# A Mamba block's back half kept with channels on the partitions

## What is computed

```python
u = layernorm(x, ln_w, ln_b); zxbcdt = u @ in_proj_w.T      # z 1024, xBC 1280, dt 16
dt = softplus(dt + dt_bias)                                 # one per token and head
xBC = silu(depthwise_conv4(xBC) + conv_b)                   # xs 1024, B 128, C 128
# per token: state = state*exp(dt*A) + (dt*x) B^T ; y = state C   (16 heads of 64 channels)
y = y + D * xs
y = y * silu(z)
y = y * rsqrt(mean(y*y) + EPS) * gamma
out = x + y @ out_proj_w.T
```

## Time and profile before

| | us |
|---|---|
| median of 3 runs | 3517.11 |
| lowest, highest | 3514.15, 3523.29 |
| the profiled execution, its own time | 3522.4 |
| its span, first to last instruction | 3521.1 |
| mean granted TensorE clock, share of full | 0.98 |

### The profile page before, as it was taken

The page is one execution under the profiler, slowest core; times in us unless marked ns, Lnnn a source line. Parts: engine busy times, 40 slices in busy tenths (PEclk is TensorE's granted clock), DMA queues, the critical chain, the costliest instruction groups (busy, mean ns, idle before and its releaser), DMA issues.

```text
span 3521.1 us, 63878 instructions
## 1 busy us (share of the span) xinstructions
PE 3307.2 (94%) x24154; PEld 1911.8 (54%) x24154; DVE 2695.3 (77%) x4854; ACT 2583.8 (73%) x4698; POOL 1812.2 (51%) x1355
## 2 busy tenths in 40 slices
PE   6799999999999999999769999999999999999997
PEld 4455555555555555555425555555555555555554
DVE  6688878788788798889867676776777777777764
ACT  6888888888998888887537656577666766666664
POOL 1233334433243442423447887876665775566655
PEclk9899999999999999999879999999999999999999
DMA  5344443445443534443367576787676877667664
GB/s 165 97 115 114 120 107 93 112 121 129 112 107 87 124 109 127 117 115 79 77 149 152 104 128 110 128 152 143 123 136 118 151 142 123 120 127 136 119 113 68
DMA packets 687315, 419.41 MB, mean 119 GB/s; under 512 B 566583, under 2 KB 603831, under 8 KB 676768
## 3 DMA queue, kind: packets, MB, share of 16 engines
q1 hardware_dynamic: 630688, 312.58, 40.1%
q0 software_dynamic: 56320, 102.75, 16.7%
HBM read 176.00 MB, written 101.71 MB: 79 GB/s over the span
## 4 chain that ended last, share of the span: by engine, by line
PE 75%; DVE 6%; DMA 6%; ACT 4%; issue 4%; POOL 3%; SPq 1%; another core or an unknown queue 0%; ACTq 0%; POOLq 0%; DVEq 0%
PE pair L1236 9%; PE pair L1311 9%; PE pair L1359 8%; PE pair L1281 8%; PE pair L1468 7%; PE pair L1321 6%; PE pair L1375 4%; PE pair L1390 3%; PE pair L1437 2%; PE pair L1436 2%; PE pair L1301 2%; PE pair L1292 2%; PE pair L1406 2%; DMA yT<-yhl 2%; PE pair L1456 1%
## 5 line engine op out<-in xcount | busy, mean ns | idle before, releaser
L1616 DVE SCALAR_TENSOR_TENSOR cv<-raw,taps,cv 128x512 f32<-128x512 f32 x480 | 433.0, 922 | 34.6 <-ACT cv L2010 31.1
L1861 DVE TENSOR_REDUCE smx<-pair 128x2 f32<-128x514 f32 x512 | 349.3, 685 | 55.8 <-PE pair L1406 53.2
L2281 POOL TENSOR_TENSOR ph<-pf,ph 128x1024 f16<-128x1024 f32 x128 | 291.5, 2277 | 185.8 <-ACT ph L2146 185.3
L1236 PE MATMUL pair<-xhT,whi 128*128 128x512 f16 x1280 | 382.2, 380 | 2.7 <-DVE yb L1686 1.0
L1311 PE MATMUL pair<-ohi,yT 128*128 128x512 f16 x1024 | 321.3, 386 | 26.3 <-DMA yT<-yhl 24.3
L2140 ACT ACTIVATE pf<-pair 128x1024 f32<-128x1024 f32 x256 | 261.8, 1023 | 113.9 <-PE pair L1437 95.4
L1281 PE MATMUL pair<-zhi,xhT 128*128 128x512 f16 x1024 | 327.3, 381 | 0.9 <-ACT btok L2030 0.4
L2040 ACT ACTIVATE de<-de,cum 128x128 f32<-128x128 f32 x1024 | 309.1, 388 | 0.4
L2146 ACT CAST ph<-pf 128x1024 f16<-128x1024 f32 x256 | 267.0, 1043 | 4.6 <-PE pair L1456 0.2
L2286 POOL TENSOR_TENSOR ohl<-of,ohl 128x256 f16<-128x256 f32 x256 | 209.8, 825 | 112.1 <-ACT ohl L2153 110.5
L1321 PEld LDWEIGHTS pair<-xdt,de 128*128 128x128 f32 x2048 | 241.3, 194 | 18.6 <-issue 12.5
(11 more groups left out here) (267 smaller groups left out, 9894.3 us busy)
## 6 DMA issues: line engine op xcount, KB each, us to landing
de<-cum SPq DMA_DIRECT2D x64, 1024.0 KB, 4.8
rows<-rowt SPq DMA_DIRECT2D x16, 1040.0 KB, 7.8
xin<-x SPq DMA_DIRECT2D x16, 1024.0 KB, 7.5
y<-xin SPq DMA_DIRECT2D x16, 1024.0 KB, 5.1
y<-ob POOLq DMA_DIRECT2D x64, 256.0 KB, 5.0
qb<-qa SPq DMA_DIRECT2D x32, 512.0 KB
rbc<-rank SPq DMA_DIRECT2D x63, 256.0 KB
wst<-wkv SPq DMA_DIRECT2D x32, 256.0 KB
```

Source lines behind the costliest of these rows:

```text
L1236: ins = pe.matmul(bk[:], w[:, k, ws], xt[:, ha, k, :], start=n == 0, stop=n == 3 * KD - 1)
L1616: ve.scalar_tensor_tensor(c_[:], r_[:, t:t + BLK], taps[:, ct, t:t + 1], c_[:], ALU.mult, ALU.add).then_inc(done, 1)
L1861: ve.tensor_reduce(smx[:, qt, 2 * h2:2 * h2 + 2], sc[:, :, 0:NK + 1], AX.X, ALU.max)
L2281: po.tensor_tensor(p_[:, 1], f[:], p_[:, 0], ALU.subtract).then_inc(S.plp, 1)
```

## The change

The back half keeps channels on the partitions. The intra product takes xdt of a head as the stationary operand (64 columns) and the decay matrix as the moving one, and two heads go to the two halves of the array's columns and of PSUM's partitions. z and inter exchange their operands. exp(cum) now varies along the free axis, so it comes by two broadcast DMAs per chunk (`ecb_in`) and one exp on ScalarE (`ecb`), into `ecb`. y is split before the norm, so `square`, `mean_` and `root` no longer stand ahead of the split; the DMA transpose `gate` is gone, and proj reads `ghl` directly. The sum of squares over the channels is a tree of three additions on GpSimd and one matmul with a single moving column (`norm`); its root scales the projection's output. The D term goes from VectorE to GpSimd, from `xsT`; the first tap from ScalarE to VectorE; the residual `skip` from ScalarE to GpSimd. `open_` leaves B out in the last chunk of a sequence. `state` moves ahead of intra. The planner's costs and dependences follow.

```diff
-          "POOL": {"low_p", "o_low", "weight_low", "row_low", "xw", "decayed", "y_skip"}}
+          "POOL": {"low_p", "o_low", "weight_low", "row_low", "xw", "decayed", "dxs", "y_skip", "tree"}}
...
 def back(i):
             if ch:
                 yield ("proj", ch - 1)
                 yield 5.18
+                yield ("norm", ch - 1)
+                yield 0.35
+            if not last and not ends(ch):
+                yield ("state", ch)
+                yield 1.72
             yield ("intra", ch)
-            yield 3.55
+            yield 1.95
...
 def z(ch, j):
-                n = 0
-                for k in range(KD):
-                    for ha, w in ((0, zhi), (0, zlo), (1, zhi)):
-                        pe.matmul(pz[:], xt[:, ha, k, cs], w[:, k, j * 512:(j + 1) * 512], start=n == 0, stop=False)
-                        n += 1
-                pe.matmul(pz[:], ones[:], z_bias[:, j * 512:(j + 1) * 512], start=False, stop=True).then_inc(S.z_mm, 1)
+                for m in range(KI // 2):
+                    ws, o, n = slice((KI // 2 * j + m) * P, (KI // 2 * j + m + 1) * P), pz[:, m * P:(m + 1) * P], 0
+                    for k in range(KD):
+                        for ha, w in ((0, zhi), (1, zhi), (0, zlo)):
+                            pe.matmul(o, w[:, k, ws], xt[:, ha, k, cs], start=n == 0, stop=False)
+                            n += 1
+                    ins = pe.matmul(o, z_bias[:, ws], ones[:], start=False, stop=True)
+                ins.then_inc(S.z_mm, 1)
 def inter(ch):
-                for j in range(2):
-                    ins = pe.matmul(pi[:, j * 512:(j + 1) * 512], xs[:, KI + 1, cs], sf[:, j * 512:(j + 1) * 512], start=True, stop=True)
+                for k in range(KI):
+                    ins = pe.matmul(pi[:, k * P:(k + 1) * P], sf[:, k * P:(k + 1) * P], xs[:, KI + 1, cs], start=True, stop=True)
 def intra(ch):
                 for h in range(NH):
-                    ins = pe.matmul(pw[:, h * HD:(h + 1) * HD], de[ch % 2][:, h, :], xdt[:, h, :], start=True, stop=True)
+                    k, a = divmod(h, 2)
+                    ins = pe.matmul(pw[a * HD:(a + 1) * HD, k * P:(k + 1) * P], xdt[:, h, :], de[ch % 2][:, h, :], start=True, stop=True)
+            def norm(ch):
+                q.wait_ge(S.tree, 3 * (ch + 1))
+                pe.matmul(bank("norm", ch)[:, 0:1], ysq[:, 0, :], upper[:, P - 1:P], start=True, stop=True).then_inc(S.nm_mm, 1)
 # VectorE
+            def tap0(i, ct):
+                ve.tensor_scalar(c_[:], r_[:, 0:BLK], taps[:, ct, 0:1], conv_bias[:, ct:ct + 1], ALU.mult, ALU.add).then_inc(S.cv0, 1)
-            def dxs_(ch):
-                ve.tensor_tensor(dxs[:], p3, d_bc[:].unsqueeze(2).to_broadcast([P, NH, HD]), ALU.mult).then_inc(S.dxs, 1)
 def y_low(ch):
-                ve.scalar_tensor_tensor(yhl[:, 1, :], yb[:].rearrange("p h d -> p (h d)"), yn[:, 2:3], yhl[:, 0, :],
-                                        ALU.mult, ALU.subtract).then_inc(S.yl, 1)
+                ve.scalar_tensor_tensor(ghl[:, 1], yb[:], GS, ghl[:, 0], ALU.mult, ALU.subtract).then_inc(S.yl, 1)
 # ScalarE
+            def ecb_(ch):
+                q.wait_ge(S.ecb_in, 32 * (fed(ch) + 1))
+                ac.activation(ecb[:], ecb[:], ACT.Exp).then_inc(S.ecb, 1)
 def square(ch):
-                ac.activation(yhl[:, 0, :], yf, ACT.Square, accum_out=yn[:, 0:1]).then_inc(S.sq, 1)
+                ac.activation(ysq[:], yb[:], ACT.Square).then_inc(S.sq, 1)
 # GpSimd
+            def skip(i, c):
+                po.tensor_tensor(xin[:, c, :], xin[:, c, :], xn[:], ALU.add).then_inc(S.skip, 1)
+            def dxs_(ch):
+                q.wait_ge(S.nm_mm, ch)
+                po.tensor_tensor(ysq[:], xsT[i % 2][:, 0:KI, c * P:(c + 1) * P], d_ch.unsqueeze(2).to_broadcast([P, KI, P]), ALU.mult).then_inc(S.dxs, 1)
+            def tree(ch):
+                q.wait_ge(S.sq, ch + 1)
+                po.tensor_tensor(ysq[:, 0:4], ysq[:, 0:4], ysq[:, 4:8], ALU.add).then_inc(*tree_own.up())
+                po.tensor_tensor(ysq[:, 0:2], ysq[:, 0:2], ysq[:, 2:4], ALU.add).then_inc(*tree_own.up())
+                po.tensor_tensor(ysq[:, 0], ysq[:, 0], ysq[:, 1], ALU.add).then_inc(*tree_own.up())
 # SyncE
-            def gate(ch):
-                sp.dma_start_transpose(yT[:], yhl[:].rearrange("p h d -> p (h d)")).then_inc(S.yT, 16)
+            def ecb_in(ch):
+                q.wait_ge(S.yi, fed(ch))
+                for a in range(2):
+                    sp.dma_start(ecb[a * HD:(a + 1) * HD], heads[a].partition_broadcast(HD)).then_inc(S.ecb_in, 16)
```

More of the change, by code:

```diff
@@ L36 @@
 WS = 64.0
+GS = 8.0
 MS = 16.0
@@ L498, in arrange_steps @@
         elif name == "proj":
-            add("PE", 5.18, step, [("gate", a), ("wout_low", KI - 1)], [("single", [("proj_out", a)])])
+            add("PE", 5.18, step, [("y_low", a), ("wout_low", KI - 1)], [("single", [("proj_out", a)])])
+        elif name == "norm":
+            add("PE", 0.35, step, [("tree", a)], [("single", [("mean", a)])])
         elif name == "rank_in":
@@ L530, in arrange_steps @@
             two = (i, c - 2) if c > 1 else (i - 1, CK - 2 + c)
-            add("ACT", 0.81, ("xn", i, c), [("stat2", i)] + [last((name, *before)) for name in ("low", "row_low", "xh")])
+            add("ACT", 0.81, ("xn", i, c), [("stat2", i)] + [last((name, *before)) for name in ("low", "row_low", "xh", "skip")])
             add("ACT", 0.62, ("row_high", i, c), [("xn", i, c), last(("rows_out", i - 1))])
@@ L578, in arrange_steps @@
         if opens(ch):
-            add("DVE", 1.22, ("y2", ch), [("intra", ch), ("dxs", ch), ("wout_low", KI - 1), last(("y_low", ch - 1))])
+            add("DVE", 1.22, ("y2", ch), [("intra", ch), ("dxs", ch), ("wout_low", KI - 1), last(("y_low", ch - 1)), last(("square", ch - 1))])
         else:
-            add("DVE", 1.22, ("y_in", ch), [("inter", ch), ("cum_exp", i), ("y_low", ch - 1)])
+            add("SP", 0.8, ("ecb_in", ch), [("cum_store", i), ("slice_low", len(PIECES) - 1), last(("y_in", ch - 2 if opens(ch - 1) else ch - 1))], extra=ECB_LANDS)
+            add("ACT", 1.05, ("ecb", ch), [("ecb_in", ch)])
+            add("DVE", 1.22, ("y_in", ch), [("inter", ch), ("ecb", ch), ("y_low", ch - 1), ("square", ch - 1)])
             add("POOL", 2.7, ("y_skip", ch), [("y_in", ch), ("dxs", ch)])
@@ L788, in back @@
                     yield ("z", ch + 1, j)
-                    yield 3.02
-                if not ends(ch):
-                    yield ("state", ch)
-                    yield 1.72
+                    yield 2.96
     plan.append(("x_in", 0))
@@ L815, in make_plan @@
     record.append(("proj", NCH - 1))
+    record.append(("norm", NCH - 1))
     record.append(("slots",))
@@ L908, in __init__ @@
         self.xs = sem("xs")
-        self.cum_mm, self.cum, self.ec, self.cumT_mm, self.cumT, self.cum_out = (
-            sem(s) for s in ("cum_mm", "cum", "ecum", "cumT_mm", "cumT", "cum_out"))
+        self.cum_mm, self.cum, self.cumT_mm, self.cumT, self.cum_out = (
+            sem(s) for s in ("cum_mm", "cum", "cumT_mm", "cumT", "cum_out"))
+        self.ecb_in, self.ecb = sem("ecb_in"), sem("ecb")
         self.bc = two("bc_in")
@@ L920, in __init__ @@
             sem(s) for s in ("intra_mm", "y_intra", "y_gated", "square", "mean_sq", "root"))
-        self.yh, self.yl, self.yT, self.o_mm, self.o = (sem(s) for s in ("y_high", "y_low", "yT", "o_mm", "o"))
+        self.yh, self.yl, self.tree, self.nm_mm, self.o_mm, self.o = (sem(s) for s in ("y_high", "y_low", "square_tree", "norm_mm", "o_mm", "o"))
         self.acc_out = two("o_out")
@@ L1130, in program @@
             "cum": lambda i: [(S.cum, i + 1), (S.cumT, i + 1)],
-            "open": lambda ch: [(S.dxs, ch + 1), (S.btok, ch + 1)],
+            "open": lambda ch: [(S.xdt, ch + 1)] + ([] if ends(ch) else [(S.btok, kept(ch) + 1)]),
             "gram": lambda ch: [(S.gm, ch + 1)],
@@ L2286, in norm_o @@
                 po.tensor_tensor(o_[:, :, 1, hs], of[h % 2][:], o_[:, :, 0, hs], ALU.subtract).then_inc(S.olo, 1)
-            does = {"pow1": pow1, "pow2": pow2, "row_low": row_low,
-                    "xw": xw_, "decayed": decayed, "y_skip": y_skip, "root": root, "o_add": o_add, "mamba_done": mamba_done, "attention": attention,
+            does = {"pow1": pow1, "pow2": pow2, "row_low": row_low, "skip": skip,
+                    "xw": xw_, "decayed": decayed, "dxs": dxs_, "y_skip": y_skip, "tree": tree, "root": root, "o_add": o_add, "mamba_done": mamba_done, "attention": attention,
                     "weight_low": weight, "set_early": set_early, "gather": gather, "qscore": qscore,
@@ L2438, in stored @@
                     q.wait_ge(S.res_out[j], 16 * ITEMS * QT // 2)
-            does = {"prep": prep, "slice_in": slice_in, "wout_in": wout_in, "x_in": x_in, "turn": turn, "gate": gate,
+            does = {"prep": prep, "slice_in": slice_in, "wout_in": wout_in, "x_in": x_in, "turn": turn, "ecb_in": ecb_in,
```

180 lines of the change are left out of this document (93 added, 87 removed).

## The result

The changed kernel takes 3624.69 us (median of 4, 3621.19 to 3642.78) against 3520.2 for the kernel before in the same session: ratio 1.0303, 95% interval 1.0267 to 1.0338. It is 3% slower, where I had forecast 0.7% faster.

The account below looks back on a forecast made before the run. TensorE bounds the kernel at 25.94 us per chunk; after the change VectorE, stopped by GpSimd, would at 25.5. Saving 0.44 in 54 chunks (-24), start -7 and tail +7 take 3522.4 to 3498; the median, 5.3 lower, is 3493 (3448 to 3560).

Parts of the forecast that it names:

- TensorE's sum: TensorE's own work per chunk: intra -1.56, z +0.21, norm +0.28 and small terms, -1.05 us in all, so 24.9 needed.
- Rivals 3 and 4: TensorE: intra's column parts don't overlap, about 3554, chance 0.04; narrow z matmuls have a floor, about 3612, chance 0.03.
- 24.6 / 0.965 = 25.5 us per chunk: Chunk length in the steady part: VectorE's need with stops, 24.6 us, divided by its reachable busy share.
- 96.5%: Share of time VectorE can be busy, taken from 19.5 of 20 us late in the stage with the ranking on it.
- the 23.1 from below: Lower bound of VectorE's need per chunk: 21.2 - 0.2 + 2.1 us, at 0.4 per added us on GpSimd.
- rival 1: Steady chunks: TensorE stays the bound and nothing else is late; 24.9 us per chunk, 3453 us, chance 0.20.
- the new waits: TensorE's norm waits for the tree, state for xw; 2 to 4 us per chunk if uncovered, no separate charge.
- Tap 0: First convolution tap, moved from ScalarE to VectorE: 0.42 us each, 2.42 per chunk, +1.0 us per chunk on VectorE.
- GpSimd's three new jobs: D product 1.89, skip 1.15 and tree 2.2 us per chunk on GpSimd: +5.25 that collides with VectorE.
- Start: Before 170 us: ScalarE loses ten first taps and some skips while TensorE waits for silu; -7 us, bounds 0 and -12.
- Tail: From 1578 us, VectorE is the bound: 8 chunks with 2.1 more stretch, 1.25 less dxs; +7 us, bounds 0 and +15.
- Rival 2: VectorE and GpSimd stop each other nearly always: VectorE needs 26.2, chunk 26.7 us, 3565 in all, chance 0.15.

Follow-up runs that it names:

- i_best6: Changed kernel with squares summed by eight small TensorE matmuls, skip sum on ScalarE, D loaded as one row, order replanned: 3501.63 us, ratio 0.9966.
- e_tiny: Changed kernel, same order, with GpSimd's D product, residual addition and tree additions cut to one column, so most of those sums are left out: 3548.07 us, ratio 1.0095.

## Why the prediction was wrong

**TensorE's sum was right.** Forecast -1.05 us per chunk; the budgets give -0.8 for the changed kernel and -1.0 for i_best6, each good to some 0.3. (The 24.9 counted TensorE's 0.36 us of idle time as work.) Intra on two column parts 1.99 (1.95 forecast), z's matmuls 0.056 each (0.056), inter 1.79 (1.76), norm 0.14 (0.28). Rivals 3 and 4 are out.

**The step that failed** is the one from VectorE's need to the chunk: "24.6 / 0.965 = 25.5 us per chunk". The need itself was not too low. VectorE's busy time, stops included, was 730.16 / 30.9 = 23.6 us per chunk, a whole us under my 24.6 and nearer to the 23.1 from below. But it was busy for 85% and not for 96.5%, and a chunk took 27.69 us. The 96.5% came from the earlier trace rows, where the ranking, 32 operations that wait for nothing but each other, fills every gap. I had taken the slowest engine's need as what sets the chunk. With "nothing else is late" in rival 1 and "I charge them in the 25.5" for the new waits, I had priced latency at nothing. TensorE's idle time rose by 1.7 us per chunk.

What makes TensorE late is a result that comes late in another engine's list, at whatever share that engine is busy. The wait of 2.65 us before 919 shows it for the stops: some 5 us of them lie on the way to xdt. The wait of 5.48 us before 816 has another source, ScalarE's full list. i_best6 has VectorE busy for 87% of the window, more than the changed kernel, and only 0.85 us idle on TensorE, so the share alone says little. That such lists can't work ahead is my reading; no run changes that alone.

**What was not in the sum at all** is the clock. Of before I had read 1.00 and kept it. With TensorE's waits of 1.6 to 5.5 us it came to a mean of 0.97, another 0.8 us per chunk. I ought to have asked what follows when TensorE stops being the bound.

**Mis-sized terms.** Tap 0: 0.42 from a copy, measured 0.54 where nothing stops it and 0.80 on average. GpSimd's three new jobs: 5.25 forecast, 7.2 with their own stops (tree 3.6 against 2.2). Start: -7 forecast, +8 measured. ScalarE's relief was there, with TensorE's wait for the first silu at 8.1 us after 21.7; but the two small loads of D cost 9 and stood in the diff, and the wait at L1232 (L1221 before) grew from 11.8 to 21.5. Tail: +7 forecast, +8 measured, but as +17 up to the last chunk's mask and -9 behind it, so the agreement is in part luck.

**The order.** I took each engine's list as given and costed only what is in it. For the same work the lists tried here differ by 7 to 53 us and once by 92; I had forecast a gain of 24. As a budget, and not as a proof, the loss of 104 us can be written as 77 for GpSimd's work in the order that it had, less some 50 for TensorE's saving (0.9 in 54 chunks), and 77 for the rest: the start, the tail, and the idle time and clock that the new dependences and their order bring. An order made for it gave 53 back to e_tiny. The parts are not independent, since each was measured with the others in place.

**Rival 2**, GpSimd against VectorE, at 3565, named the right pair of engines and had the right sign, and was 60 us short. Its quantity was wrong too: it wanted VectorE at 26.2 us per chunk and was to decide above 25.0, and VectorE was at 23.6. Of its signs, TensorE's idle time of over 1 us per chunk came, and mostly from VectorE. Like the forecast it priced neither the waits of the lists nor the clock. I gave it 0.15. Only 0.24 of each us on GpSimd reached the chunk, but 0.24 of 5.25 was already more than TensorE's whole saving.

What stays open is why one order runs better than another; no run here isolates a rule for it.
